# First attention of a fused two-layer block: queries of two batches projected together in every second step, the third chunk's values in that place in the steps between

## The reference

```python
q = (queries @ Wq + bq).reshape(N, L, H, D)
k = (keys @ Wk + bk).reshape(N, S, H, D)
v = (values @ Wv + bv).reshape(N, S, H, D)
sm = jnp.einsum('nlhd,nshd->nlhs', q, k) / math.sqrt(D)
sm = jax.nn.softmax(sm, axis=1)
attn = jnp.einsum('nlhs,nshd->nlhd', sm, v).reshape(N, L, H * D)
return attn @ Wo + bo
...
x = x + jnp.tanh(g_xattn[0]) * _L0_xattn_ref(_layernorm(x, axis=-1), ctx_1024, ctx_1024, ...)
```

## Time and profile before

| | |
|---|---|
| median of 3 runs | 1221.6 us (1221.46 to 1227.03) |
| the profiled execution's own time | 1220.75 us |
| its span, first to last instruction | 1218.9 us |
| PE busy | 1148.4 us, 94% of the span |
| DVE busy | 625.8 us, 51% |
| ACT busy | 474.6 us, 39% |
| POOL busy | 391.0 us, 32% |
| mean granted TensorE clock | 0.984 |

### The profile page before, as it was taken

One profiled execution on the slowest core, in us unless ns is written; L12 is line 12 of the kernel. 1 busy time (PEld: TensorE's weight loads), 2 busy tenths in 40 slices (PEclk: granted clock), 3 DMA queues, 4 the chain that ended last, 5 costly groups with the idle time before them and its releaser, 6 DMA issues. The chain is left out here.

```text
span 1218.9 us, 28926 instructions
## 1 busy us (share of the span) xinstructions
PE 1148.4 (94%) x11273; PEld 886.6 (73%) x11273; DVE 625.8 (51%) x1501; ACT 474.6 (39%) x1114; POOL 391.0 (32%) x413
## 2 busy tenths in 40 slices
PE   6999999977999999998999999999988999999998
PEld 4767777755999999985565665666654589999975
DVE  5777777775210101037977777668767512122226
ACT  3545555522333333324544444454454133333321
POOL 3666766642222222131001011010011245555520
PEclk9999999977999999999999999999999999999999
DMA  6011011405999999731021001000000469999965
GB/s 184 24 27 38 27 35 34 138 8 179 392 326 323 327 332 330 277 111 48 2 88 33 14 21 34 13 9 7 4 9 21 167 217 352 353 352 351 343 220 169
DMA packets 64391, 180.92 MB, mean 148 GB/s; under 512 B 10176, under 2 KB 36608, under 8 KB 55808
## 3 DMA queue, kind: packets, MB, share of 16 engines
q1 hardware_dynamic: 55088, 156.40, 37.4%
q0 software_dynamic: 8064, 22.03, 5.0%
q10 hardware_dynamic: 1104, 0.64, 0.2%
HBM read 163.11 MB, written 15.93 MB: 147 GB/s over the span
## 5 line engine op out<-in xcount | busy, mean ns | idle before, releaser
L2334 ACT ACTIVATE ex_hT<-kept_psum,ex_w 128x128 f32<-128x128 f32 x464 | 132.7, 369 | 294.5 <-PE kept_psum L2389 294.5
L2389 PE MATMUL kept_psum<-ex_xT,ex_w 128*128 128x128 f32 x1856 | 222.5, 276 | 0.0
L2296 DVE TENSOR_TENSOR ex_yt<-kept_psum,ex_b 128x256 f32<-128x256 f32 x84 | 35.7, 425 | 353.6 <-PE kept_psum L2400 353.6
L2389 PEld LDWEIGHTS kept_psum<-ex_xT,ex_w 128*128 128x128 f32 x1856 | 215.6, 193 | 0.2
L2400 PE MATMUL kept_psum<-ex_w,ex_hT 128*128 128x256 f32 x928 | 213.9, 379 | 0.0
L2400 PEld LDWEIGHTS kept_psum<-ex_w,ex_hT 128*128 128x128 f32 x928 | 170.1, 190 | 19.7
L2262 POOL DMA_INDIRECT ex_results<-ex_yt,ex_to_row x84 | 82.8, 986 | 254.6 <-DVE ex_yt L2296 254.6
L1289 ACT ACTIVATE at_probs<-kept_psum 120x800 f32<-120x800 f32 (+2 forms) x128 | 101.2, 842 | 88.3 <-PE kept_psum L1464 88.3
L1101 DVE TENSOR_REDUCE at_negmax<-kept_psum 100x2 f32<-100x722 f32 x128 | 115.4, 901 | 0.0
L570 ACT ACTIVATE at_probs<-kept_psum 120x800 f32<-120x800 f32 (+1 forms) x96 | 80.1, 836 | 73.6 <-PE kept_psum L693 73.5
L412 DVE TENSOR_REDUCE at_negmax<-kept_psum 120x8 bf16<-120x800 f32 (+1 forms) x96 | 90.5, 985 | 23.6 <-PE kept_psum L684 23.2
(11 more groups left out here) (256 smaller groups left out, 1679.1 us busy)
## 6 DMA issues: line engine op xcount, KB each, us to landing
ex_w<-in_pack_in SPq DMA_DIRECT2D x32, 1028.0 KB, 5.9
ex_w<-in_pack_out SPq DMA_DIRECT2D x32, 1024.0 KB, 7.6
ex_w<-in_pack_in SPq DMA_DIRECT2D x52, 514.0 KB, 5.3
ex_w<-in_pack_out SPq DMA_DIRECT2D x52, 512.0 KB, 5.9
at_ctx<-in_ctxT SPq DMA_DIRECT2D x31, 361.0 KB, 3.6
ex_normed<-ex_xhat SPq DMA_DIRECT2D x16, 200.0 KB
ex_w<-ex_results SPq DMA_DIRECT2D x6, 400.0 KB
ex_sw<-in_L_ffn_sW SPq DMA_DIRECT2D x2, 1024.0 KB
```

The lines of the kernel that those rows point to most:

```text
L2334: last = act.activation(hT[t % N][:, c, :], ps_h[:, (t * U + u) % N, i * P:(i + 1) * P], ACT.Gelu, bias=w1[t % N][:, B1 + c:B1 + c + 1])
L2389: last = pe.matmul(ps_h[:, (t * U + u) % N, i * P:(i + 1) * P], w1[t % N][:, c * ff + f:c * ff + f + P], xT[t % N][:, c, :], start=(c == 0 ...
```

## The change

In odd steps t = 1, 3, ... 13 TensorE transposes batches t+1 and t+2 and projects both with one set of four program matmuls, 200 columns wide instead of 100. In even steps from 2 on there is neither a transpose nor a query projection, and the values of the third chunk stand where the query projection stood, between the two shifts of chunk 0, instead of behind them. Batch 1 is still projected alone in step 0. The ring's uses become xT, xT, key0, query, value2, key1, sum, value01, out in odd steps, and key0, value2, key1, sum, value01, out in even ones. ScalarE copies a pair of queries out with four activations of 2x100 in place of eight of 100. VectorE normalises batches t+2 and t+3 in even steps, and none in odd ones. Queries lie in four buffers where there were two.

```diff
-    ring = opening + [(n, t + off) for t in range(B + 1) for n, off in ORDER if on(t + off)]
+    def queried(t):
+        return range(1, 2) if t == 0 else range(t + 1, t + 3) if t % 2 == 1 and t + 2 < B else range(0)
+    def queries(b):
+        return b + 1 if b < 2 else b // 2 + 2
+    def used(n, off, t):
+        return queried(t) if n == "xT" else queried(t)[:1] if n == "query" else [t + off] if on(t + off) else []
+    ring = opening + [(n, b) for t in range(B + 1) for n, off in ORDER for b in used(n, off, t)]
...
-                if t + 2 < B:
+                if t % 2 == 0 and t + 3 < B:
                     normed(t + 2)
+                    normed(t + 3)
...
             for i in range(KC):
+                by_batch = ring_bank("query", b)[:, i * n * T:(i + 1) * n * T].rearrange("p (b t) -> p b t", t=T)
                 for a in range(2):
-                    last = act.activation(qz[b % 2][:, i, a, :], ring_bank("query", b)[:, i * T:(i + 1) * T], ACT.Identity,
+                    last = act.activation(qz[:, b % 4:b % 4 + n, i, a, :], by_batch, ACT.Identity,
                                           bias=bqm[:, i, a:a + 1], scale=own[:, a:a + 1])
...
         for t in range(B + 4):
+            for b in queried(t):
+                take_xT(b)
             if on(t + 1):
-                take_xT(t + 1)
                 take_k(t + 1, 0)
             if on(t):
                 exponents(t, 0, (0,))
-            if on(t + 1):
-                take_q(t + 1)
+            if queried(t):
+                take_q(queried(t))
...
-                    last = pe.matmul(bank[:, i * T:(i + 1) * T], wq[:, c, i * P:(i + 1) * P], xT[b % 2][:, c, :],
+                    last = pe.matmul(bank[:, i * n * T:(i + 1) * n * T], wq[:, c, i * P:(i + 1) * P], xT[:, b % 2:b % 2 + n, c, :],
                                      start=(c == 0), stop=(c == KC - 1))
...
+            for b in queried(t):
+                transposes(b)
             if on(t + 1):
-                transposes(t + 1)
                 project_k(t + 1, 0)
             if on(t):
                 shift(t, 0, 0)
-            if on(t + 1):
-                project_q(t + 1)
+            if queried(t):
+                project_q(queried(t))
+            elif on(t + 1):
+                project_v(t + 1, (2,))
             if on(t):
                 shift(t, 0, 1)
-            if on(t + 1):
+            if queried(t) and on(t + 1):
                 project_v(t + 1, (2,))
             if on(t):
                 scores(t, 1)
```

More of the change, by code:

```diff
@@ L234, in attend0 @@
     xhat = [m.sb(f"xhat{i}", [T, D]) for i in range(2)]
-    xT = [m.sb(f"xT{i}", [P, KC, T]) for i in range(2)]
-    qz = [m.sb(f"qz{i}", [P, KC, 2, T]) for i in range(2)]
+    xT, qz = m.sb("xT", [P, 2, KC, T]), m.sb("qz", [P, 2 * 2, KC, 2, T])
     kT = [m.sb(f"kT{i}", [P, KC, S]) for i in range(2)]
@@ L545, in take_xT @@
             act.wait_ge(ready["xT"], b + 1)
-            need(act, ready["query"], b - 1)
-            act.activation(xT[b % 2][:, :, :], ring_bank("xT", b)[:, 0:KC * T].rearrange("p (c t) -> p c t", c=KC), ACT.Copy).then_inc(taken["xT"], 1)
+            need(act, ready["query"], queries(b - 2) if b > 1 else 0)
+            act.activation(xT[:, b % 2, :, :], ring_bank("xT", b)[:, 0:KC * T].rearrange("p (c t) -> p c t", c=KC), ACT.Copy).then_inc(taken["xT"], 1)
         def take_k(b, i):
@@ L553, in take_k, with take_q @@
             act.activation(kT[b % 2][:, i, :], ring_bank(name, b)[:, 0:S], ACT.Identity, bias=bks[:, i:i + 1]).then_inc(taken[name], 1)
-        def take_q(b):
-            act.wait_ge(ready["query"], b + 1)
+        def take_q(bs):
+            b, n = bs[0], len(bs)
+            act.wait_ge(ready["query"], queries(b))
             act.wait_ge(masks_set, 4)
-            need(act, scores_ready, NJ * (b - 1))
+            need(act, scores_ready, NJ * (bs[-1] - 3))
             for i in range(KC):
+                by_batch = ring_bank("query", b)[:, i * n * T:(i + 1) * n * T].rearrange("p (b t) -> p b t", t=T)
                 for a in range(2):
-                    last = act.activation(qz[b % 2][:, i, a, :], ring_bank("query", b)[:, i * T:(i + 1) * T], ACT.Identity,
+                    last = act.activation(qz[:, b % 4:b % 4 + n, i, a, :], by_batch, ACT.Identity,
                                           bias=bqm[:, i, a:a + 1], scale=own[:, a:a + 1])
@@ L593, in scalar @@
         consts.squash(act)
-        take_q(0)
+        take_q(range(1))
         for t in range(B + 4):
+            for b in queried(t):
+                take_xT(b)
             if on(t + 1):
-                take_xT(t + 1)
                 take_k(t + 1, 0)
@@ L624, in into @@
                 before, at = ring[n]
-                pe.wait_ge(taken[before], at + 1)
+                pe.wait_ge(taken[before], queries(at) if before == "query" else at + 1)
             return ring_bank(name, b)
@@ L642, in project_k, with project_q @@
             last.then_inc(ready[name], 1)
-        def project_q(b):
+        def project_q(bs):
+            b, n = bs[0], len(bs)
             bank = into("query", b)
-            pe.wait_ge(taken["xT"], b + 1)
+            pe.wait_ge(taken["xT"], bs[-1] + 1)
             for i in range(KC):
                 for c in range(KC):
-                    last = pe.matmul(bank[:, i * T:(i + 1) * T], wq[:, c, i * P:(i + 1) * P], xT[b % 2][:, c, :],
+                    last = pe.matmul(bank[:, i * n * T:(i + 1) * n * T], wq[:, c, i * P:(i + 1) * P], xT[:, b % 2:b % 2 + n, c, :],
                                      start=(c == 0), stop=(c == KC - 1))
@@ L669, in scores @@
                 pe.wait_ge(taken["key1"], t + 1)
-                pe.wait_ge(taken["query"], t + 1)
+                pe.wait_ge(taken["query"], queries(t))
             turns, routes = pair_at(t), pair_at(t - 1)
@@ L684, in scores @@
                     last = pe.matmul(score_pair(t, j, strip // 2)[0:r, strip % 2, i * 2 * T:(i + 1) * 2 * T], kT[t % 2][rows, i, s0:s0 + r],
-                                     qz[t % 2][rows, i, :, :], start=(i == 0), stop=False, skip_group_check=True)
+                                     qz[rows, t % 4, i, :, :], start=(i == 0), stop=False, skip_group_check=True)
             last.then_inc(scores_ready, 1)
@@ L737, in tensor @@
         pe.wait_ge(wq_loaded, 32)
-        project_q(0)
+        project_q(range(1))
         pe.wait_ge(wv_loaded, 32)
```

## The result

The changed kernel takes 1238.86 us (median of six runs, 1232.64 to 1241.87), the kernel before 1221.7 us in the same rounds: a ratio of 1.0122, with an interval of 1.0104 to 1.0139, about +15 us (the medians as they stand differ by 17.2). The profiled execution took 1239.34 us (span 1237.6, against 1218.9). 1230.5 was forecast, and 1238.86 lies above the range given (1221.5 to 1236).

A forecast was written before the change was run, and what follows sets the result against it. TensorE was taken to set the pace, busy 237.25 of 247.00 us. Odd steps' 7.5 us and even steps' 2.0 made +9.5 on 1220.75 us; adjusted to the median, 1230.5 us was forecast, range 1221.5 to 1236.

The forecast's parts named there:

- the mechanism: First attention: odd steps wait for a PSUM bank, even steps lose to VectorE and GpSimd excluding each other; +9.5 us.
- the sum: Whole kernel: 7.5 us from odd steps plus 2.0 from even ones, added to the profiled 1220.75 us.
- The odd steps: Seven steps gain a transpose, a wider projection and a wait of the first keys: +1.07 us each, 7.5 in all.
- the ring's bank: Odd steps: keys need the first transposes' PSUM bank and wait for ScalarE's copy, 0.33 us with the hand-over.
- A wide instruction: Query projection in odd steps: 0.172 us per instruction at 200 columns, 1.38 us for eight.
- Steps 6, 10 and 12: GpSimd's earlier halve holds VectorE's router normalisations, so TensorE's shift of chunk 2 comes late: +0.93 us each, +2.8.
- the collision: Even steps: GpSimd's halve of chunk 1 starts before VectorE's two router normalisations, which then stand still; +0.93 us per step.
- The other even steps: Step 2 -1.10 us, step 14 -0.6, steps 4 and 8 +0.3 each, step 0 +0.33.
- The third rival: Even steps: GpSimd holds small VectorE products too; +1.66 us in three steps, whole +13.6, 1234.5 us; chance 0.20.
- the tie: Steps 6, 10 and 12: VectorE's last small product starts 0.06 us behind GpSimd's halve, too close to work out.
- The first rival: Even steps: VectorE and GpSimd do not collide, so odd steps' loss is given back; +1.3 us, 1222 us; chance 0.20.
- arrives at the end whole: Stages behind the first attention run after it on the same data, so each microsecond gained or lost there reaches the total.

The follow-up runs named there:

- e2: Changed kernel with both transposes of a pair in one PSUM bank and one ScalarE copy for both: 1230.82 us, ratio 1.0058.
- e3: Changed kernel with VectorE's two normalisations of x moved from even to odd steps, except the first two pairs: 1227.49 us, ratio 1.0028.
- e12: Changed kernel with four one-column activations ahead of ScalarE's first copy of queries, meant to delay the first scores: 1235.96 us, ratio 1.0102.
- e1: Changed kernel where, in even steps from 4 on, GpSimd's halve of chunk 1 waits for both router normalisations: 1225.78 us, ratio 1.0027.
- e5: Kernel before with VectorE's half of the change alone, both normalisations in even steps: 1226.31 us, ratio 1.0020.
- e8: Changed kernel with one of step 0's two normalisations moved behind maxima 2: 1233.19 us, ratio 1.0086.
- e6: Kernel before with only the added GpSimd wait of e1: 1220.65 us, ratio 0.9980.
- e7: Changed kernel run again without an edit: 1237.50 us, ratio 1.0115.
- e4: Changed kernel with the edits of e1, e2 and e3 together: 1221.71 us, ratio 0.9987.
- e11: Kernel of e8 with four one-column activations ahead of ScalarE's first copy of queries, to delay the first scores: 1234.78 us, ratio 1.0100.

## Why the prediction was wrong

The direction and the mechanism inside the steps were right, the size was short, and the step that failed is the sum. Point by point:

**The odd steps (+1.07 each, 7.5).** They measured +1.15 in steps 3, 7, 11 and 13. The keys start 0.82 us behind the transposes, where 0.8 was named, and e2 shows that the ring's bank makes them wait: -0.5 us without it. A wide instruction takes 1.36 / 8 = 0.170 us, forecast 0.172. The missing 0.08 is the keys themselves, 135.21 - 133.89 = 1.32 us against 1.24, for which no term stood. In e2, directly behind the transposes again, they take 1.24 us; in the changed kernel's even steps, directly behind scores 0, 1.32 us. Steps 5 and 9 are longer by 0.9 at full clock (16.86 in e3 and e12).

**Steps 6, 10 and 12 (+0.93 each).** Measured +1.04, with the places as forecast: 2.67 and 1.03 us (forecast 2.68 and 1.03). The 0.11 us above are mostly the keys' 0.08 again. e1 and e3 each remove the collision, and with it the loss; e5 shows that VectorE's half alone does not bring it. This part is shown.

**The other even steps.** Step 2 gave back 1.32 (forecast 1.10), step 14 1.02 (0.6), step 0 took 0.46 more (0.33). Step 4 took 0.35 at full clock (17.25 in e8 and e12; forecast 0.3), step 8 0.90 against 0.3, near its bound of 1.0. In all the even steps are +2.5, forecast +2.0.

**The third rival** wanted the last small product held by GpSimd. The forecast itself had that product start 0.06 us behind GpSimd and yet left it unheld. In step 6 it ran in 0.16 us, 0.06 us ahead of GpSimd: the tie went the other way, and +1.66 did not come. That is luck: the keys' 0.08 us, which had no term, made GpSimd so much later, and without it the order could have been the reverse. That small products are held at all is true, and e6 shows it again, 0.81 against 0.15 us. The first rival, no collision, is excluded by the 2.61 us.

**The step that failed is the sum.** It added changes of step length and took TensorE's clock as given. The mechanism measures 7.6 + 2.5 = +10.1 us against 9.5 (step 0 as it ran, its end at half clock included). The rest of the +13.94 is 3.85 us of clock: step 1 took 18.12 against 15.71 (e1, e8), step 4 18.29 against 17.25, step 5 17.27 against 16.86. The granted clock stood at half, the 1.2 GHz level, for 6.8 us from the end of step 0 into step 1, 0.6 us behind step 0's wait, and for 3.4 us behind step 4's wait, from 97.1 on. These are the two waits in TensorE's timeline, and the stretches behind them (PEclk is the granted clock):

```profile
31.66 0.55 PE L707 MATMUL kept_psum<-at_negmax,at_identb 120*120 120x400 bf16 x2 [1.91 <-DVE at_negmax L421]
...
96.56 0.55 PE L707 MATMUL kept_psum<-at_negmax,at_identb 120*120 120x400 bf16 x2 [2.49 <-DVE at_negmax L421]
```

```profile
core 0: us, PE busy (x) PEld busy (x) DVE busy (x) ACT busy (x) POOL busy (x), PEclk, DMA share, GB/s
33.41:39.00 5.59, 5.50 (x27) 3.44 (x27) 3.15 (x5) 1.63 (x4) 4.49 (x5) 0.50 0.00 0
39.20:51.53 12.33, 12.33 (x167) 9.22 (x166) 7.19 (x16) 6.69 (x12) 6.06 (x5) 1.00 0.04 5
97.20:100.40 3.20, 3.20 (x18) 2.11 (x20) 2.32 (x9) 1.67 (x2) 0.06 (x1) 0.50 0.46 150
```

No term and no rival spoke of it. The three runs of this kernel (e7's with them) with the mean clock of before, 0.984 to 0.986, took 1232.1 to 1234.5 us, inside the range given; the median did not.

Outside the attention the profiled pair differs by 4.8 us more, for which the sum had no term either: by it a microsecond of the attention "arrives at the end whole". 1.2 us of it are later first scores, which moved between 14.36 and 15.70 in these kernels, mostly before anything that was edited. The other 3.6 us lie behind step 15's start. I see 0.72 us more wait for the first tile of the experts (5.04 against 4.32 us, for a DMA) and a pause of TensorE without a named cause, 1.08 us; the granted clock fell as often and as long there as before. A tie to the edit is not excluded: from step 15's start to the end the four profiles with TensorE's old order take 972.9 to 973.5 us, the ten with the new one 973.6 to 977.8. The cause stays open.

Neither item alone leads out of the range: 1220.75 + 10.1 + 3.85 = 1234.7 us, and with the 4.8 it is 1239.5, where 1239.34 was measured.

**What decides the clock stays open.** In every profile with a drop in step 1, step 0 had waited 1.91 us: four of eight profiles with that wait. None of the six with 1.59 us or less had one. In steps 4 and 8 drops came only behind waits of 2.19 us and more, but waits of 2.50 to 2.71 us also passed without. So a longer wait was there each time and was not enough. e1, e3, e4 and e12 exclude the wait alone, e11 the start time alone, and e12 both together.

## What to carry to other kernels

When a bound engine's work is shortened ahead of a point that a second engine waits for, work out which instructions of a third engine the second one will now overtake: here 1.10 us of TensorE's time gained became 1.04 us lost, because GpSimd passed VectorE instructions that had been one microsecond ahead. Where two engines exclude each other, a wait on the one that is not urgent can pay: here one added wait took about 12 us off the changed kernel (1.0122 to 1.0027), with the clock's drops that went along. And price a new wait of the busiest engine with its possible aftermath on the clock, as a second case beside the sum.

## What the runs showed of the hardware

A wait of 1.9 to 2.5 us on TensorE, which was busy for 97% of these steps before the change, was followed in some executions by 3.4 or 6.8 us at half the granted clock. One of 6.8 us cost 2.4 us (step 1), one of 3.4 us about 1.4 us (1.04 in step 4 and 0.41 in step 5 of the changed kernel; 16.65 against e4's 15.22 us in step 1 of e2), and the runs of one unchanged program so spread over 8.5 us, with mean clocks of 0.986 to 0.978.

GpSimd too is held when it comes second: its addition took 1.74 us in place of 1.63 where it met a normalisation in progress (e3). The side that comes first decides: VectorE lost 1.87 us where it came 0.13 us late (step 6 of the changed kernel), and GpSimd 0.11 us where it came second.
